# Moving the last state's output, the z projection and y's row factors to other slots and engines in a Mamba and MoE kernel on one core

## The reference, cut to what matters

```python
xz = einsum('bld,de->ble', layernorm(x), W_in);  x_in, z = split(xz, 2)
u = silu(causal_conv4(x_in) + conv_b)
dt, B, C = split(u @ W_xproj);  delta = softplus(dt @ W_dt + b_dt)
h_t = exp(delta_t * A) * h_(t-1) + delta_t * u_t * B_t      # 16 states a channel
y_t = sum over n of h_t[n] * C_t[n]
y = (y + D_skip * u) * silu(z)
x = x + layernorm(y @ W_out)
x = x + layernorm(shared(layernorm(x)) + sum of 2 of 8 experts, weighted by their softmax)
```

## Time and profile before

| | |
|---|---|
| median of 3 runs | 2431.92 us (2430.57 to 2432.0) |
| the profiled execution | 2430.07 us, its span 2428.1 us |
| DVE busy | 2228.7 us (92%) |
| PE busy | 2073.8 us (85%) |
| POOL busy | 1906.6 us (79%) |
| ACT busy | 1601.1 us (66%) |
| TensorE's granted clock, mean | 0.938 |

### The profile page before, as it was taken

One profiled execution on the slowest core, in us unless ns is written; L12 is line 12 of the kernel. 1 busy time (PEld: TensorE's weight loads), 2 busy tenths in 40 slices (PEclk: granted clock), 3 DMA queues, 4 the chain that ended last, 5 costly groups with the idle time before them and its releaser, 6 DMA issues. The chain is left out here.

```text
span 2428.1 us, 29696 instructions
## 1 busy us (share of the span) xinstructions
PE 2073.8 (85%) x8960; PEld 1322.8 (54%) x8960; DVE 2228.7 (92%) x3176; ACT 1601.1 (66%) x2358; POOL 1906.6 (79%) x1566
## 2 busy tenths in 40 slices
...
DMA packets 92943, 134.23 MB, mean 55 GB/s; under 512 B 12000, under 2 KB 42976, under 8 KB 92784
## 3 DMA queue, kind: packets, MB, share of 16 engines
...
## 5 line engine op out<-in xcount | busy, mean ns | idle before, releaser
L753 DVE TENSOR_TENSOR_SCAN h<-d_a,carry,d_bu 128x512 f32<-128x512 f32 x1024 | 1262.0, 1267 | 35.8 <-ACT d_a L602 35.4
L987 POOL TENSOR_TENSOR d_bu<-delta_u,b_rows 128x1024 f32<-128x1024 f32 x512 | 1202.3, 2357 | 5.1 <-DMA b_rows<-b_rows_hbm 0.9
L602 ACT ACTIVATE d_a<-delta,a_neg 128x512 f32<-128x512 f32 x1024 | 696.4, 689 | 622.2 <-DVE h L753 620.2
L445 PE MATMUL ht<-ident,h 128*128 128x128 f32 x4096 | 618.1, 295 | 116.8 <-DVE y_t L763 111.8
L445 PEld LDWEIGHTS ht<-ident,h 128*128 128x128 f32 x4096 | 503.7, 151 | 367.5 <-issue 132.0
L763 DVE SCALAR_TENSOR_TENSOR y_t<-ht,c_t,y_t 128x512 f32<-128x512 f32 x960 | 665.5, 734 | 2.8 <-PE ht L445 2.6
L509 PE MATMUL ring<-x_t,w_gate_sb 128*128 128x512 f32 x640 | 329.1, 641 | 20.6 <-ACT delta L718 19.1
L516 PE MATMUL ring<-x_t,w_up_sb 128*128 128x512 f32 x640 | 296.4, 606 | 23.0 <-ACT silu_gate L671 22.8
L536 PE MATMUL dn<-w_down_sb,hidden 128*128 128x256 f32 x1280 | 304.3, 381 | 13.2 <-POOL hidden L1045 13.2
L1040 POOL TENSOR_TENSOR hidden<-silu_gate,up 128x512 f32<-128x512 f32 x160 | 204.3, 1277 | 135.8 <-ACT up L675 77.9
L536 PEld LDWEIGHTS dn<-w_down_sb,hidden 128*128 128x128 f32 x1280 | 236.0, 190 | 74.8 <-issue 31.8
...
## 6 DMA issues: line engine op xcount, KB each, us to landing
b_rows<-b_rows_hbm SPq DMA_DIRECT2D x256, 256.0 KB, 3.5
coef_rows<-coef_rows_hbm SPq DMA_DIRECT2D x128, 256.0 KB, 3.5
...
```

The lines of the kernel that those rows point to most:

```text
L445: last = nc.tensor.transpose(HT[q % HTS][:, j * P:(j + 1) * P], H[:, (NS * c + n) % HS, j, a * P:(a + 1) * P], IDN[:, :])
L602: nc.scalar.activation(DA[i % DAS][:, :], DL[:, r, j, :], ACT.Exp, scale=ANEG[:, j, n:n + 1]).then_inc(ex.sem, 1)
L753: nc.vector.tensor_tensor_scan(H[:, (NS * s + n) % HS, j, :], DA[(n * J + j) % DAS][:, :], BU[:, (2 * n + j // 2) % 4, j % 2, :], CARRY[:, ...
L987: nc.gpsimd.tensor_tensor(BU[:, (2 * n + h) % 4, :, :], DU[:, 2 * h:2 * h + 2, :], BB[:, n % 2, :].unsqueeze(1).to_broadcast([P, 2, T]), A ...
```

## The change

Five things move, and no arithmetic is left out.

The last state, q = 60 to 63. VectorE no longer adds it. ScalarE scales the transposed state by C into a tile `YB` of its own (`last_state`, L631 in the new kernel), in slots 0 and 1 among the decays, and TensorE transposes `YB` into the same PSUM banks as `y_t`, on top of it (`transpose_last`), so that the sum is made there.

y's way. The transposes stand in slot 1 (blocks 0 and 1) and slot 4 (blocks 2 and 3) instead of slot 2; D*u in slots 3 and 5 instead of 3; the first x_in in slot 3 instead of 4. GpSimd's gate stands ahead of the `d_bu` of slot 4, not behind it.

z. All four blocks are projected in slot 9 and copied raw to SBUF by ScalarE in slots 8 and 9 of its list; one group of four silus follows in slot 60. The silu of u's blocks 0 and 1 moves from slot 8 to 7. In the step ahead of the first scan the silus of z stand in slot 11.

x's transposes move from slot 0 of a step to slot 58 of the step before, the copies from slot 1 to slot 59.

Statistics. The moments of the MoE's output in slot 60 come behind the two additions of that slot. Its row factors move from slot 60 to slot 0 of the next step, behind the first `d_bu` of that chunk; its normalisation from slot 0 to 2; the sum with the stream from 7 to 8. The moments of x are taken in slots 26, 32, 36, 42, with the closing step in 46 (before: 32, 32, 42, 42), their row factors in 46 (44). The head of the convolution (`before_chunk`) moves from slot 1 to slot 15 of the step before.

```diff
-        HF = sb("hidden", [P, 2, T])
-        UP = sb("up", [P, 2, T])
+        UP_HF = sb("up_hidden", [P, 4, T])
+        UP, HF = UP_HF[:, 0:2, :], UP_HF[:, 2:4, :]
+        YB = UP_HF
...
-        XIN_PE, TAP0_ACT, CONV = (4, 4, 7, 8), (4, 5, 8, 8), (6, 7, 10, 11)
-        YD_PE, YD_DVE, Y_GATE, OUT_PE = 2, 3, 4, (5, 5, 6, 6)
-        Y_POOL = 7
+        XIN_PE, TAP0_ACT, CONV = (3, 4, 7, 8), (4, 5, 8, 8), (6, 7, 10, 11)
+        YD_PE, YD_DVE, Y_GATE, OUT_PE = (1, 4), (3, 3, 5, 5), 4, (5, 5, 6, 6)
+        Y_POOL = 8
...
-        XA_STATS, XA_RSTD, XA_NORM = (32, 32, 42, 42), 44, 49
+        XA_STATS, XA_MEAN, XA_RSTD, XA_NORM, XT_PE, XT_ACT = (26, 32, 36, 42), 46, 47, 50, 58, 59
...
-        Z_PE, Y_STATS = (9, 9, 60, 61), 60
-        SILU = {8: [("u", 0), ("u", 1), ("z", 0), ("z", 1)], 11: [("u", 2), ("u", 3)], 62: [("z", 2), ("z", 3)]}
+        Z_PE, Z_ACT, Y_STATS = 9, (8, 8, 9, 9), 60
+        U_EARLY, HEAD_POOL = 7, 15
+        SILU = {11: [("u", 2), ("u", 3)], 60: [("z", j) for j in range(J)]}
+        SILU_FIRST = {11: SILU[11] + SILU[60]}
...
+            def transpose_last(s, a, js):
+
+                pe.wait_ge(*added(s - 1, SLOTS - NT + a))
+                for j in js:
+                    step = nc.tensor.matmul(yd_bank(j)[:, a * P:(a + 1) * P], YB[:, a, j * P:(j + 1) * P], IDN[:, :],
+                                            start=False, stop=(a == NT - 1), is_transpose=True,
+                                            skip_group_check=True)
+                    if a == NT - 1:
+                        step.then_inc(full["yd"].sem, 1)
...
-                        pe.wait_ge(sz.sem, sz.at(s + 1, 2))
+                        pe.wait_ge(z_raw.sem, z_raw.at(s + 1))
...
+            def last_state(c, r, q):
+
+                a = q - SLOTS + NT
+                act.wait_ge(ht_full.sem, ht_full.at(c, q + 1))
+                act.wait_ge(down.sem, down.at(c - 1))
+                nc.scalar.activation(YB[:, a, :], HT[q % HTS][:, :], ACT.Copy, scale=CT[:, r, a, NS - 1:NS])\
+                  .then_inc(y_last.sem, 1)
...
+                    if ffn and t == 0:
+                        last_state(s - 1, o, SLOTS - NT)
+                        last_state(s - 1, o, SLOTS - NT + 1)
+                    if ffn and t == 1:
+                        last_state(s - 1, o, SLOTS - NT + 2)
...
-                    for q in ADDS_LATE.get(t, ()):
-                        if ffn:
-                            add_state(s - 1, o, q)
```

More of the change, by code:

```diff
@@ L408, in body @@
                             transpose_state(s, q)
[L409 removed]
+                    for q in LAST_Q.get(t, ()):
                         if ffn:
@@ L477, in ffn_part @@
                 c = s - 1
-                if t == YD_PE:
-                    for j in range(J):
-                        transpose_y(s, lo, j)
+                for half in range(2):
+                    if t == YD_PE[half]:
+                        for j in (2 * half, 2 * half + 1):
+                            transpose_y(s, lo, j)
+                        for a in range(NT):
+                            transpose_last(s, a, (2 * half, 2 * half + 1))
                 for j in range(J):
@@ L650, in body @@
                         normed("xa", s + 2, XA, XA)
+                    if exists(lo + 2) and t == XT_ACT:
+                        for k in range(KM):
+                            act.wait_ge(full["xt"].sem, full["xt"].at(s + 2, k + 1))
+                            act.wait_ge(full["z"].sem, full["z"].at(s + 1))
+                            nc.scalar.activation(XT[:, k, :], ring_bank("xt", k)[:, :], ACT.Copy)\
+                              .then_inc(xt.sem, 1)
             def ffn_part(s, lo, o, t):
```

97 lines of the change are left out of this document (50 added, 47 removed).

## The result

The median of the kernel before is 2431.24 us here (2429.9 to 2432.0), that of the changed kernel **2396.03 us** (2395.94 to 2396.95): a ratio of 0.9857, 95% interval 0.984 to 0.9874. The forecast was 2399, with a range of 2366 to 2422. The profiled spans are 2428.1 and 2394.3 us, 33.8 us apart.

A forecast was written before the change was run, and what follows sets the result against it. VectorE's own work was taken to bound the kernel, with TensorE and ScalarE binding at scan 14 after the change. A step gains 0.8 + 0.6 + 0.8 = 2.2 us, 14 steps 31, with the ends 33: 2399 us, range 2366 to 2422.

The forecast's parts named there:

- Slot 60: End of each step: two additions fill VectorE's 1.20 us wait for the last MoE product; gain 0.8 us (0.3 to 1.2).
- Middle slots: Slots 26, 36, 46: x's moments cover three VectorE waits of 0.19 us; gain 0.6 us a step (0 to 0.6).
- The boundary: From T (start of slot 0's scan) to scan 14, bound by TensorE and ScalarE: gain 1.8 us, 0.8 after clock loss.
- The clock: TensorE's lower clock at the boundary delays its chain to the last z: loss 1.0 us a step (0 to 5.5).
- The head: Start of the kernel: scan 0 some 5.5 us later, offset by waits that go; net 0 us (-3 to +3).
- Step 15 and the tail: Kernel's end: step 15, without x_in and set by GpSimd's chain, gains 2.5 us; the tail gains 0.5.
- Rival A: At the boundary TensorE keeps up: a step gains 3.6 to 4.8 us, total 2363 to 2380 us; chance 16%.
- Rival C: Clock stays low from slot 61 to the first x_in every step: 2.3 us a step lost, 2462 us; chance 10%.
- Rivals B and D: B: new boundary waits eat VectorE's savings, 2419 to 2430 us, 12%; D: additions return as scaling waits, 2412 us, 2%.

The follow-up runs named there:

- e4: Changed kernel with the closing step of x's moments in slot 44 instead of 46: 2386.88 us.
- e2: Kernel before with one part of the change, the moments of the MoE's output behind the additions of slot 60: 2431.01 us.
- e3: Kernel before with only x's moments, their closing step, row factors and normalisation moved to the changed kernel's slots: 2428.4 us.
- e7: Changed kernel with z's blocks 2 and 3 projected for only 128 of the 512 tokens: 2394.77 us.
- e6: Changed kernel with five more idle 512-column matmuls on TensorE, four in slot 60 and one in slot 62: 2386.04 us.
- e1: Changed kernel with VectorE adding the last state again in slots 0 and 1, all else staying moved: 2437.45 us.
- e11: The kernel of e1 with five idle matmuls added on TensorE in slots 60 and 62: 2436.08 us.

## Why the prediction was right, and where its steps were off

**Slot 60** was right in size and cause: 0.78 us gained (0.8 foretold), the rest held back by GpSimd's wait for the closing step of x's moments (0.97 us, where up to 0.9 of delay was foretold and 0.4 taken; e4 removes it). What the step didn't see is that this gain isn't free by itself: e2 shows that in the kernel before GpSimd gives it back at o's factors. The prediction had the condition as a remark on o's factors ("GpSimd got rid of the convolution's head"), without the 2.35 us of the sum with the stream, and not as the price of the whole term. (In the working and in the change's description x's row factors are put in slot 46; they stand in 47, and the normalisation in 50.)

**Middle slots**: the three waits of 0.19 went as foretold, 0.57 us; alone (e3) they are worth only 0.2 a step. What the prediction didn't see is that TensorE's clock can make waits in the middle of a step too. It read one boundary of the kernel before and took 143.75 us for the length of every step from 2 to 14. Three of them were 0.3 to 1.0 us longer, and two of these had such waits (0.36 and 0.53 us in the one of 144.7). In the changed kernel one step in three loses 0.5 us there.

**The boundary.** Foretold was scan 14 at T+39.2 without a loss by the clock and T+40.2 with it. It stands at T+39.33, T+39.53 and T+40.28 in the three kinds of step. The chain by which this was worked out was right up to z: D*u of slot 5 waited (0.27 to 0.75 us, 0.7 foretold), `d_bu` for scan 4 came late (T+7.0 against T+6.8), and o's factors wait 0.30 us, less than the 0.7 foretold, since the sum with the stream left GpSimd's list there too. Its last part named the wrong link (e7): from block 1 of z on it is ScalarE's own list that takes the time up to decay 14, and the rest of z is projected in about the same time. The time of T+39.2 that came of it was right all the same: with the clock up scan 14 stands at T+38.97 (e6).

**The clock was the term mis-sized.** 1.0 us was taken in every step. Against e6 it costs 0.4, 0.6 and 1.3 us at scan 14 in the three kinds of step, 0.7 in the mean. Against the kernel before, scan 14 came 1.8, 1.6 and 0.8 us earlier, 1.4 in the mean, and not 0.8; in the kernel before it stood at T+41.1 in nearly all steps, wherever the clock was low. So a step gained 143.88 - 141.01 = 2.87 us in the mean instead of 2.2, which is 37 us in 13 steps instead of 29. The prediction took one size of loss for all steps. The Trainium skill's rule ("TensorE: Matmul & The Clock Gate", part 4) would have the clock low all through the transposes. The runs agree in part: with sparse transposes alone the clock stands at 0.50 (window 1170 to 1174), but by 1176.94 it had come back in a stretch where TensorE had run nothing but transposes since 1165.93, the last of them without a gap from 1173.59 on. In every step from 2 to 14 the clock was back before the first x_in began.

**The head was wrong** by 4.8 us: 0 foretold, 4.8 lost. (Step 1 gained 1.2, as foretold: 2.2, less 1 for the cold TensorE.) The step named the wait of 3.12 us that would go and the wait of 2.38 that would shrink. The first did go, but scan 0 came 5.9 us later (5.5 foretold), the second was replaced by three waits (0.97, 0.74 and 1.08 us), and the silus of slot 60 in step 0 weren't priced at all. The prediction itself had said that without moments and additions they hold up scan 63; step 0 is that case, at 1.71 us.

**Step 15 and the tail** gave 0.1 instead of 3.0 us: 1.4 instead of 2.5 in the step, and a loss of 1.3 instead of a gain of 0.5 behind the last scan. The gates in front of two `d_bu` hold up scan 8 for 3.56 us, a wait that the gain put down to this step ("the chain is GpSimd's") left out. Why the tail lost was not tried; its new waits are those at D*u, 5.41 and 1.06 us, where one of 0.76 us stood before.

So the sum, 33 us against 33.8, is closer than its parts, and that is luck: the 13 steps gave 8.7 us more, the head 4.8 less and the end 2.9 less. Rival A, a gain of 3.6 to 4.8 us a step, came true in no step; the short ones gained 3.2 and lost 0.4 to the clock. Rival C's first x_in at the lower clock is what e1 and e11 have, and they are slower than before. Rivals B and D are excluded by the 2.87 us.
